# Attention and expert kernel: first score rows as one full-precision product, put last, and all V copies on VectorE

## The reference

```python
h = _layernorm(x, axis=-1) * (1 + ca) + sa
x = x + ga * _L0_attn_ref(h, W_Q, W_K, W_V, W_out, b_out)
h = _layernorm(x, axis=-1) * (1 + cb) + sb
x = x + gb * _L0_ffn_ref(h, W1, b1, W2, b2, Wr, br)
# attention
q, k, v = (jnp.einsum('bsd,dhk->bshk', resid, W) for W in (W_Q, W_K, W_V))
scores = jnp.einsum('bqhc,bshc->bhqs', q, k) / sqrt(64)
probs = softmax(where(causal_mask, MASK_FILL, scores), axis=-1)
z = jnp.einsum('bhqs,bshc->bqhc', probs, v)
out = jnp.einsum('bqhc,chd->bqd', z, W_out) + b_out
# experts
weights = softmax(top 2 of (xf @ Wr + br))
h = gelu(xf @ W1[e] + b1[e]);  out = sum over e of weights[:, e] * (h @ W2[e] + b2[e])
```

## Time and profile before

| what | value |
|---|---|
| median of 3 runs | 1879.13 us (1876.46 to 1879.55) |
| the profiled execution | 1881.74 us, span 1879.9 us |
| granted PE clock in it | 0.998 |
| PE, DVE, ACT, POOL busy | 99%, 87%, 83%, 39% |
| attention | about the first 1130 us |
| 128 head pairs | 7.96 to 10.88 us each, rows shown below for some |

### The profile page before, as it was taken

The page is one execution under the profiler, slowest core; times in us unless marked ns, Lnnn a source line. Parts: engine busy times, 40 slices in busy tenths (PEclk is TensorE's granted clock), DMA queues, the critical chain, the costliest instruction groups (busy, mean ns, idle before and its releaser), DMA issues.

```text
span 1879.9 us, 50582 instructions
## 1 busy us (share of the span) xinstructions
PE 1865.9 (99%) x15334; PEld 1431.6 (76%) x15334; DVE 1642.9 (87%) x4388; ACT 1558.2 (83%) x3664; POOL 729.7 (39%) x1212
## 2 busy tenths in 40 slices
PE   8999999999999999999999999999999999999999
PEld 6777777777777777777777777888888888888887
DVE  7898888888888888888888888989998999999998
ACT  6988988988998998998988988777777777777775
POOL 3454454454454444544445442222222222222221
PEclk9999999999999999999999999999999999999999
DMA  4200000000000000000000003111111111111111
GB/s 122 69 2 1 1 1 1 1 1 1 1 1 0 1 1 0 1 1 0 1 1 1 1 2 91 52 51 51 51 51 51 51 51 51 51 51 51 51 56 51
DMA packets 42622, 50.04 MB, mean 27 GB/s; under 512 B 3160, under 2 KB 24464, under 8 KB 42512
## 3 DMA queue, kind: packets, MB, share of 16 engines
q1 hardware_dynamic: 42256, 48.41, 8.1%
q0 software_dynamic: 256, 0.53, 0.1%
HBM read 44.47 MB, written 4.46 MB: 26 GB/s over the span
## 4 chain that ended last, share of the span: by engine, by line
PE 97%; DVE 1%; ACT 1%; issue 1%; DMA 0%; SPq 0%; ACTq 0%; DVEq 0%
PE banks L605 16%; PE banks L578 13%; PE banks L592 9%; PE banks L684 6%; PE banks L686 6%; PE banks L685 6%; PE banks L703 6%; PE banks L705 6%; PE banks L704 6%; PE banks L523 6%; PE banks L525 5%; PE banks L524 5%; PE banks L627 2%; PE banks L629 2%; PE banks L628 2%
## 5 line engine op out<-in xcount | busy, mean ns | idle before, releaser
L501 POOL TENSOR_SCALAR probs<-probs,rdenom 128x512 f32<-128x512 f32 (+3 forms) x1024 | 523.9, 533 | 584.5 <-DVE rdenom L1248 584.5
L954 ACT ACTIVATE probs<-probs,neg_max 128x512 f32<-128x512 f32 (+3 forms) x1024 | 561.8, 551 | 52.0 <-DVE neg_max L1239 52.0
L1059 ACT ACTIVATE hidden<-banks,b_cols 128x512 f32<-128x512 f32 x512 | 349.5, 688 | 177.7 <-PE banks L686 177.4
L1418 DVE TENSOR_TENSOR hid_lo<-hidden,hid_hi 128x512 fp32r<-128x512 f32 x512 | 380.3, 754 | 56.8 <-ACT hid_hi L1067 42.0
L1239 DVE CUSTOM_DVE_ANT_0 probs<-banks,mask_w 128x512 f32<-128x512 f32 (+3 forms) x1024 | 427.1, 482 | 0.7 <-PE banks L578 0.7
L487 POOL TENSOR_TENSOR acc<-acc,y_w 128x512 f32<-128x512 f32 x110 | 151.4, 1377 | 462.8 <-DVE y_w L1431 461.0
L605 PE MATMUL banks<-probs_T,v_sb 128*64 128x512 f32 (+3 forms) x2048 | 304.6, 440 | 0.3 <-issue 0.3
L1232 DVE COPY probs_T<-banks 128x512 f32<-128x512 f32 (+1 forms) x256 | 232.6, 949 | 30.0 <-PE banks L592 30.0
L605 PEld LDWEIGHTS banks<-probs_T,v_sb 128*64 128x64 f32 x2048 | 136.4, 137 | 155.7 <-issue 119.4
L592 PEld LDWEIGHTS banks<-ident,probs 64*128 64x128 f32 x5120 | 171.7, 140 | 45.3 <-issue 45.3
L684 PE MATMUL banks<-h_hi,w_hi 128*128 128x512 f32 x512 | 205.8, 402 | 0.1
(11 more groups left out here) (182 smaller groups left out, 3393.3 us busy)
## 6 DMA issues: line engine op xcount, KB each, us to landing
w_rows<-w_kept SPq DMA_DIRECT2D x128, 256.0 KB, 4.5
x_all<-in_L_attn_resid_dram SPq DMA_DIRECT2D x16, 256.0 KB, 2.8
w_raw<-in_L_ffn_W_dram SPq DMA_DIRECT2D x16, 256.0 KB, 4.8
out_dram<-y_result SPq DMA_DIRECT2D x15, 256.0 KB, 2.3
v_sb<-in_L_attn_W_V_dram SPq DMA_DIRECT2D x1, 512.0 KB, 9.8
hidden<-in_L_attn_W_out_dram POOLq DMA_DIRECT2D x2, 256.0 KB, 7.7
v_sb<-in_L_attn_W_Q_dram SPq DMA_DIRECT2D x1, 448.0 KB, 6.3
v_sb<-in_L_attn_W_K_dram SPq DMA_DIRECT2D x1, 448.0 KB, 7.5
```

The costliest lines, as they stand in the source:

```text
L501: pool.tensor_scalar(part, part, rdenom[:, p % 2, 4 * h + r:4 * h + r + 1], 1.0, ALU.mult, ALU.mult)\
L954: act.activation(part, part, ACT.Exp, bias=neg_max[:, p % 2, col:col + 1], scale=-1.0, accum_out=denom[:, p % 2, col:col + 1]).then_inc(p_ ...
L1059: act.activation(hidden[:, e % 2, c, :], banks[:, c, :], ACT.Gelu, bias=b1_cols[:, e * HC + c:e * HC + c + 1]).then_inc(hid, 1)
L1418: dve.tensor_tensor(hid_lo[:, e % 2, c, :], full, hi.bitcast(F32), ALU.subtract)\
```

## The change

Row 0 of the scores (128 queries by 128 keys) becomes one plain fp32 product per head from q_full and k_full. These are new tiles that POOL makes as hi + lo of the first 128 columns (`join`), behind the normalizing of the pair two earlier. Row 0 moves from unit 1 to the end of unit 2, into banks 6 and 7 behind row 1. The semaphores count accordingly. `values_out` moves from ACT to DVE, where all V chunks of a pair are copied behind `rest_k` and ahead of `evac_T`; on ACT the exponentials of a unit are no longer interrupted.

```diff
-UNITS = [[3], [2, 0], [1]]
+UNITS = [[3], [2], [1, 0]]
-ROW_IN_BANK = {3: 0, 2: 0, 0: 384, 1: 0}
+ROW_IN_BANK = {3: 0, 2: 0, 0: 256, 1: 0}
...
-    return (h, 2 + 2 * h, 6 + h)[u]
+    return (h, 2 + h, 4 + 2 * h)[u]
...
+            q_full = sa("q_full", [P, 2, P])
+            k_full = sa("k_full", [P, 2, P])
...
+                            if not (last and p >= NP - 2):
+                                join(*after(*after(b, p)))
+
+                    def join(b, p):
+
+                        wait_alone(pool, q_lo, pair(1, b, p) + 1)
+                        pool.tensor_tensor(q_full[:, p % 2, :], q_hi2[:, p % 2, 0:P].bitcast(F32),
+                                           q_lo2[:, p % 2, 0:P].bitcast(F32), ALU.add).then_inc(q_whole, 1)
+                        wait_alone(pool, k_lo, pair(1, b, p) + 1)
+                        pool.tensor_tensor(k_full[:, p % 2, :], k_hi2[:, p % 2, 0:P].bitcast(F32),
+                                           k_lo2[:, p % 2, 0:P].bitcast(F32), ALU.add).then_inc(k_whole, 1)
+
+                    join(0, 0)
+                    join(0, 1)
...
-                            pe.wait_ge(s_masked, (2, 6, 8)[u])
+                            pe.wait_ge(s_masked, (2, 4, 8)[u])
...
                         for r in UNITS[u]:
+                            if r == 0:
+                                pe.wait_ge(q_whole, pair(1, b, p) + 1)
+                                pe.wait_ge(k_whole, pair(1, b, p) + 1)
+                                at = ROW_IN_BANK[0]
+                                for h in range(2):
+                                    own = slice(h * DH, (h + 1) * DH)
+                                    mm = pe.matmul(S_BANK[u][h][:, at:at + P], q_full[own, p % 2, :],
+                                                   k_full[own, p % 2, :], start=True, stop=True)
+                                continue
...
-                        pe.wait_ge(s_masked, pair(8, b, p) + (7, 2)[n])
+                        pe.wait_ge(s_masked, pair(8, b, p) + (6, 2)[n])
...
-                                pe.wait_ge(s_masked, done + 6)
+                                pe.wait_ge(s_masked, done + 4)
...
-                        exponentials(b, p, 1, 1, [2])
+                        exponentials(b, p, 1, 1)
...
-                        if now:
-                            values_out(b, put[0], now[0])
-                        exponentials(b, p, 1, 1, [0])
-                        if len(now) > 1:
-                            values_out(b, put[1], now[1])
                         exponentials(b, p, 0, 2)
...
-                        for n, i in zip(put[2:], now[2:]):
-                            values_out(b, n, i)
...
+                    def values_out(b, n, i):
+                        cols = slice((i // 4) % 2 * 512, (i // 4) % 2 * 512 + 512)
+                        dve.wait_ge(v_ps, 8 * b + i + 1)
+                        dve.tensor_copy(v_sb[:, i % 4, cols], V_BANK[n]).then_inc(v_done, 1)
...
+                        for n, i in zip(put, now):
+                            values_out(b, n, i)
```

More of the change, by code:

```diff
@@ L356, in adaln_moe_kernel @@
             q_lo = sem("q_lo")
+            q_whole, k_whole = sem("q_whole"), sem("k_whole")
             k_lo = sem("k_lo")
@@ L974, in half_out @@
                                        scale=gate_cols[:, 0, ds(b, 1)]).then_inc(o_half, 1)
[L976 to L979, removed]
                     def round_weights(i):
@@ L1079, in front @@
                         prev, nxt = before(b, p), after(b, p)
-                        now = chunks(p, first, last)
                         exponentials(b, p, 0, 0)
@@ L1099, in front @@
                             round_w(1, 1)
-                        put = chunk_banks(p, first, last)
-                        if now:
-                            values_out(b, put[0], now[0])
-                        exponentials(b, p, 1, 1, [0])
-                        if len(now) > 1:
-                            values_out(b, put[1], now[1])
                         exponentials(b, p, 0, 2)
@@ L1460, in rear @@
                         has_next = not (last and p == NP - 1)
+                        now = chunks(p, first, last)
+                        put = chunk_banks(p, first, last)
                         if p == 2 and not last:
```

## The result

| kernel | median us | range | profiled span |
|---|---|---|---|
| before | 1879.32 (4 runs) | 1876.46 to 1879.55 | 1879.9 |
| changed | 1932.23 (4 runs) | 1930.01 to 1932.62 | 1930.3 |

The ratio of changed to before is 1.0279, 95% interval 1.0266 to 1.0292. The forecast was 1928 us, in a range of 1903 to 1948.

The account below looks back on a forecast made before the run. PE bounds the kernel; one-chunk pairs +34.6 us, two-chunk +14.1, third +2.2, seventh -1.8, first batch's second pair +1: together +50 on 1881.74, 1932. Put on record as 1928 us, range 1903 to 1948.

Parts of the forecast that it names:

- The bound and the slack: PE bounds the span; VectorE's turned copies end 0.41 us before PE writes scores into banks 6 and 7 again.
- The loop: Weighing values on PE (W), k_hi, k_lo, V copy, turned copies, next W: 8.50 us with one chunk, against 7.96.
- Two chunks: Pairs with two V chunks: PE waits for the first V copy ahead of transposes; 9.11 us against 8.64, +0.47.
- Third and seventh pair: In each batch, third pair waits for turned copies behind gated output, +0.15 us; seventh has DVE slack, -0.11.
- Row 0's product: Two full-precision passes on PE, both heads side by side, about 0.23 us, against 0.29 for six products before.
- the case where nobody waits: Without waits PE would gain 0.11 us a pair, 14 us over 128 pairs.
- Joins: Two POOL additions a pair, 0.37 us each, with 3.0 us of cover before row 0 wants k_full: no cost.
- z_hi gets earlier by one exp, which the loop does not see: Row 0's exps come later on ACT, so z_hi starts one exp earlier; no time counted for it.
- A: Row 0 costs PE 0.46 us instead of 0.23, heads or loads one after the other: 1953 us; chance 0.10.
- B: Looser loop, V copies 0.57 us, load's 0.05 not paid: +0.40 and +0.35, 1916 us; chance 0.82 together with forecast.
- C: Faster: earlier z_hi and ACT's free time bring k_lo forward, PE's 14 us stand: 1865 us; chance 0.05.
- D: No difference: a loop of about 8.0 us, half of the V copy hidden: 1879 us; chance 0.03.

Follow-up runs that it names:

- sums_by_head_v_on_dve: sums_by_head with the V copies back on VectorE, behind k_lo, as in the changed kernel; 1930.8 us, ratio to before 1.0278.
- half_copies: The changed kernel with V copies of 256 instead of 512 columns in batches 1 to 15; 1907.6 us, ratio to before 1.0155.
- row0_twice: The changed kernel with row 0's full-precision product issued twice per head; 1959.9 us, ratio to before 1.0434.
- sums_by_head: The changed kernel with V copies on ScalarE, a pair's last exp behind ScalarE's turned copy, sums inverted head by head; 1873.0 us, ratio to before 0.9968.
- v_only: The kernel before with its V copies moved to VectorE, behind k_lo, score rows as before; 1932.8 us, ratio to before 1.0284.
- v_only_four_exps: v_only with row 0's first-head exp moved from ahead of z_hi to behind k_hi; 1921.1 us, ratio to before 1.0226.

## Why the prediction was right

**The bound and the slack: right.** PE set the length, with 0.41 us to spare at VectorE's turned copies. Row 0's new place took 0.29 of it, and the V copy then put in 0.60.

**The loop: right.** One chunk 8.48 for 8.50. sums_by_head_v_on_dve and half_copies show it by themselves.

**Two chunks: right in size, by two errors that nearly cancel.** The V copies start at 636.15 in the pair from W = 630.92 to 640.07; PE's transposes go on at 637.07, 0.24 us behind the end of the first copy, not 0.06. Changed kernel, PE:

```profile
637.07 1.18 PE L617 MATMUL banks<-ident,probs 64*128 64x64 f32 x31 [0.45 <-DVE v_sb L1267]
...
639.37 0.32 PE L603 MATMUL banks<-k_hi,q_hi 64*128 64x256 f32 x2
...
640.07 1.40 PE L630 MATMUL banks<-probs_T,v_sb 128*64 128x512 f32 x6
```

So row 1 starts 8.45 behind W where 8.33 was forecast. The turned copies, which end at 639.16, did not hold it up again, and from row 1 to the next W it is 0.70 us, not the 0.78 behind a wait. The pair lasts 9.15 for 9.11. That the total came out is in part luck.

**Third and seventh pair: right.** From W to W the third lasts 10.13 us against 9.99 before (0.15 forecast), the seventh 10.77 against 10.89 (-0.11 forecast). The batch of the table is 3.12 us longer, 4 x 0.54 + 2 x 0.47 + 0.15 - 0.11 = 3.14 forecast. The sum said 1932. The 1928 put on record took 2.6 us off because the median of before lay that far under its profiled execution, and some 1.4 for distrust in last digits, without a row for it. In the changed kernel the profiled execution (1932.18) and the median (1932.23) are alike, so the sum was the better number.

**Row 0's product: its cost right, its gain in part.** Two passes cost 0.22 to 0.23 us (row0_twice). From the start of the scores to the weighing PE takes 614.43 - 612.41 = 2.02 and 622.29 - 620.30 = 1.99 us in two pairs of sums_by_head, against 2.10 before and 1.99 forecast. With rounded products at the same place, in the pair that matches the first, it is 2.08:

```profile
616.06 0.48 PE L580 MATMUL banks<-k_hi,q_hi 64*128 64x512 f32 x2
...
618.14 2.37 PE L607 MATMUL banks<-probs_T,v_sb 128*64 128x512 f32 x16
```

So 2.02 against 2.08 is the product, 0.06, and 2.08 against 2.10 the place, 0.02: in this pair 0.08 of the 0.11. But the place also makes the third pair of each batch wait (10.15 us against 9.99), and rounded row 0 there is no faster than before (1880.1 against 1879.2). Of the 14 us that I gave to the case where nobody waits, sums_by_head brings 6.

**Joins: nothing, right, though dearer.** An addition took 463 ns, not 370; its row in the changed kernel:

```profile
L513 POOL TENSOR_TENSOR q_full<-q_hi,q_lo 128x128 f32<-128x128 f32 x128 | 59.2, 463 | 180.2 <-DVE q_lo L1228 173.9 <-DMA wr_sb<-in_L_ffn_Wr_dram 6.4
```

k_full is done at 654.01 + 0.46 in the pair above, row 0 is due at 656.71: 2.2 us of cover, where I had 3.0 less 0.4.

**"z_hi gets earlier by one exp, which the loop does not see": true and incomplete.** In v_only, where that exp still stands ahead of z_hi, the second loop ends last in three of eight pairs. The prediction did not price that loop. V copies alone cost as much as the whole change (1932.8 and 1932.2), and that is chance. Against v_only the changed kernel is 0.22 us longer in three of four one-chunk pairs (8.47 for 8.25), because row 0 no longer stands between the turned copies and row 1, and 0.12 longer in the third pair. It is 0.06 shorter in the fourth one-chunk pair, 0.34 and 0.41 shorter in the two-chunk pairs and 0.14 in the seventh. I priced the one loop that would bind after the change and not the one that would bind after half of it, so v_only missed by 19 us.

The rivals: A, dear row 0, is out by row0_twice. B, the looser loop, would have had pairs of 8.36 and 8.99 us; they last 8.47 and 9.15. C, that ScalarE's free time brings k_lo forward, is out: k_lo stays 4.63 us behind W, at PE's K product. D, half of the copy hidden, is out by half_copies.

## What to carry to other kernels

Average room on an engine says nothing of a place: find the operation that hangs on the bounding engine's own last product, and price whatever is put between it and the buffer that the bounding engine wants back. Work out every closed loop, also those a little shorter than the bound, because moving work between engines changes which one is longest, and the halves of a change need not add up: here they cost 54 and 12 us alone and 53 together. When an operation is given back to an engine, the order around it must be worked out again: with V on ScalarE it took three orders to turn 1890.9 us into 1873.0.

## What the runs showed of the hardware

A full-precision product with 64 rows, 128-column weights and 128 columns is two passes, 0.11 to 0.12 us each (row0_twice: 0.22 to 0.23 us for two more), with both heads side by side on their row halves. The loads of all four passes of row 0 are done or under way while the products ahead of them still run:

```profile
648.12 0.31 PEld L593 LDWEIGHTS banks<-k_full,q_full 64*128 64x128 f32 x4
```

They end at 648.43, and the four passes run from 648.24 to 648.62. Three rounded products of the same size cost 0.06 us more (sums_by_head and its rounded control). When VectorE's copy was what PE waited for ahead of scores, PE started 0.06 us behind its end (656.19 to 656.25 in the changed kernel); ahead of transposes 0.24 behind (637.07 there, 629.05 in v_only_four_exps). Why these differ was not tested.
